# Ahead of three waits of TensorE, transposes of the identity into unused columns of PSUM

## What is computed

```python
# layer 0: 8 heads of width 8; q, k, v from one small projection
scores = einsum('bhqd,bhkd->bhqk', q, k)
attn = softmax(scores) / sqrt(64)
# its ffn: top 2 of 8 LoRA experts (rank 16) beside a base matrix 512 x 512
# layer 1: 32 query heads, 8 key heads of width 128, q and k RMS-normed, ALiBi bias, causal
# its ffn: 512 -> 1376 -> 512 with 4-bit weights and LoRA, relu between
```

## Time and profile before

| | |
|---|---|
| runs | 1408.39, 1408.86, 1411.47 us; median 1408.86 |
| profiled execution, its own time | 1408.48 us |
| its span, first to last instruction | 1406.7 us |
| mean granted clock of TensorE | 0.989 |

### The profile page before, as it was taken

One profiled execution on the slowest core, in us unless ns is written; L12 is line 12 of the kernel. 1 busy time (PEld: TensorE's weight loads), 2 busy tenths in 40 slices (PEclk: granted clock), 3 DMA queues, 4 the chain that ended last, 5 costly groups with the idle time before them and its releaser, 6 DMA issues. The chain is left out here.

```text
span 1406.7 us, 21472 instructions
## 1 busy us (share of the span) xinstructions
PE 1344.7 (96%) x7350; PEld 1078.3 (77%) x7350; DVE 931.9 (66%) x1659; ACT 880.0 (63%) x2167; POOL 660.8 (47%) x988
## 2 busy tenths in 40 slices
PE   6898987999999999999999999999999999999997
PEld 5543345788888888888888888888888887778886
DVE  5766555667776777767677767777676777676433
ACT  6255564667776777667677767776676766663211
POOL 5233266445465555545454645555454545443311
PEclk9999999899999999999999999999999999999999
DMA  4100032102010110102020101101020202033110
GB/s 162 53 1 1 0 106 71 31 1 61 27 51 11 52 56 22 47 16 77 2 61 27 51 11 52 61 16 51 12 77 1 62 11 50 5 95 120 36 61 30
DMA packets 36028, 61.02 MB, mean 43 GB/s; under 512 B 9200, under 2 KB 13424, under 8 KB 35920
## 3 DMA queue, kind: packets, MB, share of 16 engines
q1 hardware_dynamic: 35920, 59.66, 13.6%
HBM read 49.68 MB, written 9.96 MB: 42 GB/s over the span
## 5 line engine op out<-in xcount | busy, mean ns | idle before, releaser
L947 POOL TENSOR_TENSOR RI<-SM,C 128x1 f32<-128x1 f32 x256 | 151.8, 593 | 410.3 <-ACT PB L1310 410.1
L1791 DVE TENSOR_TENSOR R<-T,R 128x512 fp32r<-128x512 f32 x288 | 198.8, 691 | 115.4 <-ACT R L1383 105.0
L1784 DVE CUSTOM_DVE_ANT_0 PB<-S,REL,SLC 128x128 f32<-128x128 f32 (+7 forms) x256 | 204.6, 813 | 82.9 <-PE S L2039 79.9
L1310 ACT ACTIVATE PB<-PB,NM 128x128 f32<-128x128 f32 (+7 forms) x256 | 198.2, 774 | 45.5 <-DVE NM L1784 44.7
L1383 ACT ACTIVATE R<-T 128x512 fp32r<-128x512 f32 x288 | 171.3, 596 | 81.1 <-PE T L2428 78.0
L948 POOL TENSOR_SCALAR PB<-PB,RI 128x128 f32<-128x128 f32 (+7 forms) x256 | 209.7, 819 | 25.2
L2428 PE MATMUL T<-C,PB 128*128 128x128 f32 x1152 | 176.0, 276 | 7.6 <-DVE R L1791 3.3
L2428 PEld LDWEIGHTS T<-C,PB 128*128 128x128 f32 x1152 | 135.7, 141 | 37.6 <-DVE R L1791 13.9
L1370 ACT ACTIVATE DQ<-DQ 128x704 f32<-128x704 int32 x128 | 97.5, 785 | 78.4 <-DVE DQ L1865 76.4
L2037 PE MATMUL WB<-R,XT 128*128 128x512 f32 (+1 forms) x268 | 105.1, 392 | 0.0
L2039 PE MATMUL WB<-R,XT 128*128 128x512 f32 (+1 forms) x268 | 103.9, 388 | 0.0
(11 more groups left out here) (311 smaller groups left out, 3501.9 us busy)
## 6 DMA issues: line engine op xcount, KB each, us to landing
RAW<-w SPq DMA_DIRECT2D x85, 256.0 KB, 2.7
DQ<-codes SPq DMA_DIRECT2D x16, 352.0 KB, 4.0
DQ<-absmax SPq DMA_DIRECT2D x16, 352.0 KB, 2.9
dequantised<-DQ SPq DMA_DIRECT2D x16, 352.0 KB, 4.1
PB<-dequantised SPq DMA_DIRECT2D x5, 512.0 KB, 3.5
PB<-x SPq DMA_DIRECT2D x8, 256.0 KB, 4.7
PB<-x_scratch SPq DMA_DIRECT2D x8, 256.0 KB, 3.7
out<-PB SPq DMA_DIRECT2D x8, 256.0 KB, 2.0
```

The lines of the kernel that those rows point to most:

```text
L947: ch.link(e.tensor_tensor(RI[:, k:k + 1], SM[:, k:k + 1], C[:, C_EXP + 5:C_EXP + 6], ALU.pow))
L1310: e.activation(pb(m, a, 0, L), pb(m, a, 0, L), ACT.Exp, scale=-1.0, bias=NM[:, k:k + 1], accum_out=SM[:, k:k + 1]).then_inc(exp_done, 1)
L1784: e.tensor_tensor_reduce(out=pb(m, a, 0, L), in0=bank[:, 0:L], in1=REL[:, TOK - L:TOK], scale=SLC[:, a:a + 1], scalar=3.0e38, op0=ALU.add, ...
L1791: e.tensor_tensor(r(o + 512, 512), bank[:, :], rf(o, 512), ALU.subtract).then_inc(t_free, 1)
```

## The change

A helper `keep_warm(bank, n)` issues n transposes of the identity (128x128) into the first 128 columns of a bank. It is called with S[0] and 10 ahead of the wait for the join of q/k block (2, 1) (place 1); with T[0] and 14 in `turn_shift(0)`, between `mring` and the wait for the shift rows (place 2); and with the bank of QT and 14 in slot 0, ahead of the waits for the transposes of q, with the ring wait of that bank ahead of it (place 3). No semaphore is raised, and what they write is overwritten by what the bank is used for next.

```diff
--- before.py
+++ after.py
@@ -2107,6 +2107,11 @@
                 e.matmul(WB[:, :], xt(m % 3 // 2, kt, t * P, P), r((WBASE_H, WBASE_L, WBASE_H)[m % 3] + c, D),
                          start=m == 0, stop=False)
 
+            def keep_warm(bank, n):
+
+                for _ in range(n):
+                    e.transpose(bank[:, 0:P], IDENT, IDENT)
+
             for what, t in LN_PE:
                 t = int(t)
                 if what == "X":
@@ -2117,6 +2122,7 @@
                     pe.wait_ge(split, W0_QK)
                     pe.wait_ge(t_free, T_A["X", (3, 3, 7)[t]] + 1)
                     qk(*QK_FIRST[t])
+            keep_warm(S[0], 10)
             pe.wait_ge(t_free, T_A["QK", 2, 1] + 1)
             qk(*QK_THEN[0])
             max0(0)
@@ -2152,6 +2158,8 @@
 
                 k = M_AT["SH", u]
                 mring(k)
+                if u == 0:
+                    keep_warm(T[k % 2], 14)
                 pe.wait_ge(shift_ready, u + 1)
                 for qb in range(4):
                     last = e.transpose(T[k % 2][:, qb * P:(qb + 1) * P], SHF[:, qb * P:(qb + 1) * P], IDENT)
@@ -2437,6 +2445,9 @@
                     elif it == "PKV":
                         project_kv(i % NT, at(g, i, "PKV"), T[AT[known, "PKV"] % 2], at(g, i // NT * NT, ("CH", "K", 1)))
                     elif it == "QK":
+                        if known == 0:
+                            ring(at(g, i, "QT"))
+                            keep_warm(T[AT[known, "QT"] % 2], 14)
                         pe.wait_ge(w_free, at(g, i, "PQ") + 1)
                         transpose_q(at(g, i, "QT"), T[AT[known, "QT"] % 2])
                         if block_of(i):
```

## The result

The changed kernel takes 1405.34 us in the median of 20 runs (from 1402.81 us up), the kernel before, beside it, 1409.95 us (20 runs, 1406.41 to 1413.45). One of the 20 runs of the changed kernel was disturbed, with 1506.03 us at a mean granted clock of 0.844, and is left out of the ratio and of all that follows. The ratio is 0.9972 with an interval of 0.9962 to 0.9982. So it is faster, by some 4 to 5 us in the first series and 6 to 7 in the second.

A forecast was written before the change was run, and what follows sets the result against it. PE was taken as the bound, at half clock behind three waits in the first 262 us. Savings of 1.58 + 0.5 + 1.62 = 3.7 us from the median 1408.86 gave 1405.2 us, range 1403.7 to 1408.9.

The forecast's parts named there:

- The waits are covered: At all three places the transposes (1.1, 1.5, 1.5 us) end before DVE releases PE, so cost nothing on the path.
- The two ring waits: Ahead of the transposes at places 2 and 3: already fulfilled when PE gets there, so passed at once.
- Place 1: Behind the q/k block join: twelve matmuls at full clock take 2.63 us instead of 4.21, saving 1.58 us.
- The gain of the first layer: Rival: the attention loop takes up the savings of places 1 and 2, leaving place 3's 1.62; 1407.2 us, chance 0.07.
- Place 3: Slot 0, transposes of q to the next slot's scores: 4.03 us instead of 5.65, saving 1.62 us.
- Place 2: Behind the shift rows: ACT starts 0.9 to 1.0 us earlier, half taken, saving 0.5 us; bounds 0 to 1.6.
- The new short wait for POOL's line 996: At place 2: PE, no longer slow, waits for POOL's multiplications where it didn't before.
- The sum: Savings at the three places, 1.58 + 0.5 + 1.62 = 3.7 us, taken from the median 1408.86 to give 1405.2 us.
- Partly elsewhere: Rival: in other executions the clock falls in stretches not covered, so the median gains about 1.85 us; 1407.0 us, chance 0.27.
- Transposes count: Transposes look like work to the clock gate; the rival that they don't count gave 1408.9 us, chance 0.10.
- Slower: Rival: transposes run at half clock and overrun the waits at places 2 and 3 by 1.8 us; 1410.6 us, chance 0.06.

The follow-up runs named there:

- e6: The change with 20, 28 and 28 transposes instead of 10, 14 and 14, against the kernel before: ratio 0.9980, median 1408.05 us.
- e5: The unedited change measured again in a second series, against the kernel before: ratio 0.9952, median 1404.11 us.
- e1: Only the transposes at places 1 and 2, none in slot 0, against the kernel before: ratio 0.9979, median 1407.53 us.
- e3: None at the three places, but transposes into VB in waits of the prologue of layer 1, against the kernel before: ratio 0.9958, median 1404.55 us.
- e2: Only the transposes at place 3 (slot 0), against the kernel before: ratio 0.9972, median 1406.04 us.
- e4: The change and the transposes of e3 together, against the kernel before: ratio 0.9928, median 1400.93 us.
- e7: The change with half as many ordinary 512-column matmuls (5, 7, 7) instead of transposes, against the kernel before: ratio 0.9952, median 1404.42 us.
- e8: The change with 5, 7 and 7 transposes instead of 10, 14 and 14, against the kernel before: ratio 0.9962, median 1404.74 us.

## Why the prediction was right, and where it was off

**The waits are covered, right.** All three groups ended before the releaser, by 1.14, 0.48 and 0.46 us (1.1, 0.5 and 0.4 predicted), and e6 shows the price when the cover is gone: nothing at place 1, 0.9 us at places 2 and 3. The two ring waits were passed at once.

**Place 1, right to the digit.** 2.63 us for the twelve matmuls, from 4.21. The gain of the first layer is not lost in it: 2.39 us arrive at slot 0 (the traces of e5 and of before), for 1.58 + 0.5 predicted, and e1 shows it in the times.

**Place 3, right.** 4.02 us where 4.03 was predicted.

**Place 2, the term that was mis-sized.** The new short wait for POOL's line 996 is there (0.28 us, at 69.19). From the transposes of the shift rows to the first scores of the loop it is 69.78 - 67.80 = 1.98 us, for 2.73 in the earlier trace rows: 0.75 less, near the 0.9 to 1.0 that I saw reach ACT. I then took only half, 0.5, out of caution about the loop; the bounds, 0 to 1.6, were wide enough for what came here. The loop takes nothing back. A later product of its values, line 2199 before (2204 in e3, 2207 in the changed kernel), shows it. Before, with 3.4 us of low clock, then e3, with 10, then the change:

```profile
...
86.54 1.07 PE L2199 MATMUL VB<-PB,L0S 128*32 128x512 f32 x8
...
```

```profile
...
88.56 1.90 PE L2204 MATMUL VB<-PB,L0S 128*32 128x512 f32 x8
...
```

```profile
...
83.88 1.85 PE L2207 MATMUL VB<-PB,L0S 128*32 128x512 f32 x8
...
```

Counted from the transposes of the shift rows (69.66 in the earlier trace rows, 69.16 in the trace of e3, 67.80) that is 16.88, 19.40 and 16.08 us. So place 2 is worth 0.8 us when the low stretch is short, and 3.3 when it is long; my upper bound, 1.6, was taken from place 1 and was wrong. Behind place 2 the clock can take longer to come back than behind the others, as e2 and e3 show (68.3 to 78 at about 0.50); in the trace of before it took no longer. The work there is scores on 32 rows and products of 32 columns; that this thin work is why it stays down was not tested.

**The sum.** 1.58 + 0.5 + 1.62 = 3.7 us. The traces of e5 and of before, which differ in their low stretches up to slot 0 only at the three places, give 4.0, the 0.3 more being place 2's. The medians differ by 4.6 in the first series and 5.7 in the second (1409.85 - 1404.11). The forecast time, 1405.2, came within 0.2 us of the median by more luck than its sum deserves: the kernel before had a median of 1409.95 in the long series, 1.1 us above that of the three runs from which I subtracted.

What the sum doesn't explain: e1, e2 and e3, too, gained more than their places give in a trace, e2 most of all (4.4 us for 1.6 at most). A single low stretch of 3.4 us is 0.0012 of mean clock, and e2's is 0.0030 above before. Longer falls behind place 2 can give some of it in e1 and the change, but not in e2 and e3, which leave place 2 as it was. Chance is possible: e2's interval reaches down to 1.7 us, and e3's to 3.7. The rival is that an edit of PE's stream by itself shifts how often the clock falls elsewhere, in the first attention above all. No run with as many fillers at a place where the clock stays up anyway was made, so this stays open. It doesn't touch the 4.0 us that the traces show at the three places themselves.

**Partly elsewhere.** This rival described what one execution does, and the profiled one of the changed kernel is an example: three falls avoided, and others in 84 to 101 and 196 to 203 us, so that it took as long as before. In the mean it isn't so: the clock rises from 0.9873 (before, with e1 to e4) to 0.9917 in the changed kernel (19 executions), and in the second series from 0.9879 to 0.9930 (e5). My doubt was whether the fall would come at the three places at all. It came at each of them in all three traces that leave it unfilled.

**Transposes count.** The stretch at 228 us in the earlier trace rows was the right row to trust. The clock stays at 1.00 where more than half of PE's work is transposes (e3, 240.85 to 245.3 us), and matmuls in their place gain no more (0.9952 both, intervals of some 0.002 either way). The rule of the Trainium skill in "TensorE: Matmul & The Clock Gate", Part 4, that the full clock doesn't engage for transposes, does not hold for this kernel's fp32 transposes, as e3, e4 and e7 show.

**Slower.** This rival's price was set too high: a group of four that takes 0.74 us is 0.19 us a transpose, not 0.21, so fourteen take 2.6 us and overrun the two waits by 0.5 and 0.6, in sum 1.1 us instead of 1.8 (1410.0 us instead of 1410.6). It would have needed the transposes to run at half clock. They ran at 0.11 us each, and the clock was 1.00 at the start of all three waits in every trace here that has them filled.

## What to carry to other kernels

Where PE is the bound, look for waits of about 2 us with a low granted clock behind them, and fill them with work into columns that nobody reads, ahead of the wait and shorter than it: here 38 transposes of 0.11 us gave 4 to 7 us, and 87 gave 9.5 (e4). Half as many gave about as much (e8), and too much costs what it overruns (e6). Judge such a change by the mean clock and the time of many executions; the one in the profile may have its falls elsewhere, and here it showed a faster kernel as slower.

## What the hardware showed beside that

- The same kernel differs by 9 to 13 us from one execution to another (1406.93 to 1415.78 us in 27, 1405.57 to 1418.25 in 24). Most of that goes with the mean granted clock: a straight line falls by 1.10 and 1.06 us for each 0.001, with correlations of -0.93 and -0.91.
- A low stretch lasted 3.4 us in each of the three traces behind place 1 and in each behind place 3, where dense work follows. Where the loop of the first attention follows it lasted from 3.4 us (behind place 2 in the kernel before) over 6.7 (84 to 91 us in the changed kernel) to 10 (68.3 to 78 in e2 and e3).
- In the loop of the first attention a shorter wait can be enough for a fall: in the profiled execution of the changed kernel the clock went down at 84 us, behind a wait of 1.40 us for DVE's line 1653 (at 83.45), when PE had been busy 1.60 of the three us before (81 to 84). It isn't always: in the kernel before PE was busy 1.59 of the three us from 83.6, with the same wait (1.41 us, until 86.11), and the clock stayed at 1.00. In the trace of e8 a rest of 1.69 us between dense work brought none.
